# A bias tile of 32 columns instead of 64: every later tile of a cross-attention kernel moves down by 128 bytes

## What is computed

```python
q = _split_heads(hidden_states @ w_q, HEADS)
k = _split_heads(text @ w_k, HEADS)
v = _split_heads(text @ w_v, HEADS)
out_text = _merge_heads(_sdpa(q, k, v))
k_ip = _split_heads(ip_h @ w_k_ip, HEADS)
v_ip = _split_heads(ip_h @ w_v_ip, HEADS)
out_ip = _merge_heads(_sdpa(q, k_ip, v_ip, mask=mask_ip))
out = (out_text + IP_SCALE * out_ip) @ w_out + b_out
out = out + residual
```

## Time and profile before

| what | before |
|---|---|
| median of 3 runs | 918.4 us |
| lowest and highest run | 918.04 and 919.05 us |
| profiled execution: device time | 918.04 us |
| profiled execution: span from first to last instruction | 916.2 us |
| TensorE busy / VectorE busy / ScalarE busy / GpSimd busy | 97% / 80% / 66% / 57% |
| mean granted share of TensorE's clock | 0.992 |

### The profile page before, as it was taken

The page is one execution under the profiler, slowest core; times in us unless marked ns, Lnnn a source line. Parts: engine busy times, 40 slices in busy tenths (PEclk is TensorE's granted clock), DMA queues, the critical chain, the costliest instruction groups (busy, mean ns, idle before and its releaser), DMA issues.

```text
span 916.2 us, 13827 instructions
## 1 busy us (share of the span) xinstructions
PE 884.4 (97%) x4685; PEld 752.8 (82%) x4685; DVE 728.9 (80%) x999; ACT 605.3 (66%) x982; POOL 525.1 (57%) x422
## 2 busy tenths in 40 slices
PE   7999879999999999999999999999999999999967
PEld 7978758888888888888888888888888888888846
DVE  6494888888797978888897979787887879797772
ACT  4465767685858577676858586775768485866651
POOL 3372647566483928475664839284756648392731
PEclk9999999999999999999999999999999999999979
DMA  8685020303030110303030301203030303010101
GB/s 278 204 278 175 23 72 1 123 1 129 1 122 1 53 75 0 122 0 129 0 122 0 119 10 40 82 0 129 0 122 0 129 0 113 1 58 1 38 20 58
DMA packets 34151, 64.79 MB, mean 71 GB/s; under 512 B 4428, under 2 KB 6604, under 8 KB 33996
## 3 DMA queue, kind: packets, MB, share of 16 engines
q1 hardware_dynamic: 32812, 61.82, 20.2%
q10 hardware_dynamic: 1312, 2.62, 0.9%
HBM read 40.84 MB, written 23.59 MB: 70 GB/s over the span
## 4 chain that ended last, share of the span: by engine, by line
PE 81%; DVE 5%; ACT 2%; POOL 1%; issue 1%; POOLq 0%; DVEq 0%
PE bank L105 22%; PE bank L107 22%; PE bank L106 22%; PE bank L874 7%; PE bank L883 4%; PE bank L884 4%; DVE o_raw L754 1%; DVE total L765 1%; DVE pT_lo L747 1%; POOL prob L552 1%; ACT oT_hi L672 0%; ACT pv_part L668 0%; DVE prob L552 0%; POOL prob L558 0%; DVE prob L558 0%
## 5 line engine op out<-in xcount | busy, mean ns | idle before, releaser
L619 POOL TENSOR_TENSOR oT_lo<-o_raw,oT_hi 128x512 fp32r<-128x512 f32 x80 | 103.1, 1289 | 248.1 <-ACT oT_hi L672 248.1
L558 POOL TENSOR_TENSOR prob<-prob,inv 128x1120 f32<-128x1120 f32 x124 | 169.8, 1401 | 8.5 <-DVE inv L767 8.5
L552 POOL TENSOR_TENSOR prob<-prob,top 128x1120 f32<-128x1120 f32 x124 | 174.6, 1438 | 0.0
L105 PE MATMUL bank<-xT_hi,wq_hi 128*128 128x512 f32 x400 | 163.5, 409 | 2.6 <-DVE qT_lo L137 2.6
L107 PE MATMUL bank<-xT_hi,wq_lo 128*128 128x512 f32 x400 | 157.2, 393 | 0.0
L105 PE MATMUL bank<-oT_hi,wo_hi 128*128 128x512 f32 x400 | 156.1, 390 | 1.1 <-POOL oT_lo L619 0.7
L106 PE MATMUL bank<-xT_lo,wq_hi 128*128 128x512 f32 x400 | 156.1, 390 | 0.0
L106 PE MATMUL bank<-oT_lo,wo_hi 128*128 128x512 f32 x400 | 155.9, 390 | 0.0
L107 PE MATMUL bank<-oT_hi,wo_lo 128*128 128x512 f32 x400 | 155.6, 389 | 0.0
L754 DVE TENSOR_TENSOR o_raw<-bank,pv_part 64x512 f32<-64x512 f32 x160 | 110.2, 689 | 49.3 <-ACT pv_part L668 45.4
L759 DVE TENSOR_REDUCE top<-prob 128x20 f32<-128x1120 f32 (+1 forms) x128 | 98.8, 814 | 43.7 <-POOL prob L607 43.4
(11 more groups left out here) (88 smaller groups left out, 1741.3 us busy)
## 6 DMA issues: line engine op xcount, KB each, us to landing
outT<-res SPq DMA_DIRECT2D x80, 256.0 KB, 6.7
xin<-in_xT SPq DMA_DIRECT2D x14, 1280.0 KB, 6.8
w_raw<-in_L_xattn_w_v SPq DMA_DIRECT2D x8, 320.0 KB, 4.3
w_raw<-in_L_xattn_w_k SPq DMA_DIRECT2D x8, 320.0 KB, 3.6
w_raw<-in_L_xattn_w_v_ip SPq DMA_DIRECT2D x8, 320.0 KB, 3.8
w_raw<-in_L_xattn_w_k_ip SPq DMA_DIRECT2D x8, 320.0 KB, 3.8
xin<-in_xT ACTq DMA_DIRECT2D x2, 1280.0 KB, 7.4
v_raw<-v_scratch SPq DMA_DIRECT2D x16, 160.0 KB, 4.3
```

The lines of the kernel that those rows point to most:

```text
L105: nc.tensor.matmul(dst, a_hi, b_hi, start=first, stop=False)
L552: ins = eng.tensor_tensor(s, s, top[:, t, n, :].unsqueeze(2).broadcast_to([P, HEADS, k1 - k0]), ALU.subtract)
L558: ins = eng.tensor_tensor(s, s, inv[:, t, n, :].unsqueeze(2).broadcast_to([P, HEADS, k1 - k0]), ALU.mult)
L619: nc.gpsimd.tensor_tensor(oT_lo[:, m, :], o_raw[:, m % 2, :], oT_hi[:, m, :].bitcast(F32), ALU.subtract).then_inc(oT_lo_done, 1)
```

## The change

`LINE` goes from 64 to 32. It is used once, as the width of `bias`, so `bias` takes 128 bytes of each partition instead of 256, and each tile behind it starts 128 bytes lower.

```diff
@@ -33,7 +33,7 @@
 GRID = 32
 GQ = 512
 GT = GQ // P
-LINE = 64
+LINE = 32
 RING = 4
 LOADS = 6
```

## The result

| | before | after |
|---|---|---|
| median of 6 runs | 918.37 us | 923.74 us |
| lowest and highest | 917.51, 919.05 | 923.10, 924.72 |
| ratio after / before, 95% interval | | 1.0057 (1.0047 to 1.0067) |
| span of the profiled execution | 916.2 us | 922.5 us |
| distance of two output matmuls, mean | 227.1 ns | 232.5 ns |

The forecast was 918.3 us in a range of 916.4 to 920.6. The change costs 5.4 us by the medians and 6.3 us by the two profiled spans.

The account below looks back on a forecast made before the run. The prediction took TensorE, busy in 97% of the span, to bound the kernel. Its terms, 0 + 0 + 0 + 0, left the profiled 918.04 us at 918.0; it took 918.3 us for the median, range 916.4 to 920.6.

Parts of the forecast that it names:

- What bounds the kernel: Whole kernel: TensorE works in 97% of the span, with gaps only in the first 6 us and at both group ends.
- The streamed tile: 1520 TensorE matmuls streaming moved oT and pT: new address costs 0, bounds 21 us less or 21 us more.
- a fixed cost of a matmul: Reading of the 14.5 or 12.3 ns each TensorE matmul takes on top of its columns: it stays after the change.
- a cost of starting in the middle of a 256-byte piece: Other reading of those 14.5 or 12.3 ns per TensorE matmul: they go when the streamed tile starts at 0 modulo 256.
- The two-run row: Setup matmul streaming two 128-column runs, each starting at 128 modulo 256: 0.12 and 0.11 us, so the start costs nothing.
- The loaded tile: 640 transposes loading prob and 320 matmuls loading v_parts: 0, from setup loads at four addresses modulo 256 reading 0.17 to 0.18 us.
- VectorE, ScalarE, GpSimd: 0: Steps of these engines on moved tiles: 0, small operands worth 2 or 3 ns, ScalarE bounded at 3%.
- transfers: 0: Loads and stores of res, w_raw, ctx_raw and v_raw: 0, with bounds of 0.6 us on both sides.
- TensorE's streams get slower: Rival: a few ns more on 1520 streaming steps; 3 ns would be 4.6 us, 923; chance 4%.
- The first rival, cheaper streams: 14 ns less on 1520 streaming TensorE steps, 21 us, 897 us; or 2 to 5 ns, 915 to 911; chance 8% together.
- How the numbers follow: Chances for the whole kernel: 79% all terms below 0.2% together, 11% faster, 10% slower; range leaves out TensorE's stream cases, 12%.
- What would show it: Signs: output matmuls still 0.228 us apart if right; 0.215 or 0.24 with queries unchanged for an address cost on TensorE.

Follow-up runs that it names:

- kernel 1: Kernel before with 128-byte pads around oT, so only oT starts at 0 modulo 256 instead of 128: 924.05 us, ratio 1.0063.
- kernel 3: Kernel before with bias 32 columns and 128-byte pads before wq_hi and res, main-block tiles from wq_hi on at 0 modulo 256: 919.72 us, ratio 1.0012.
- kernel 5: Changed kernel's layout behind bias, with wo also moved to 0 modulo 256, so oT and wo are both at 0: 917.84 us, ratio 0.9996.
- kernel 13: Kernel before with only the loaded tile wo moved to 0 modulo 256, other main-block tiles at 128: 922.70 us, ratio 1.0052.
- kernel 12: Kernel before with bias 32 columns and a pad before k_hi, streamed k at 0 modulo 256, loaded qT at 128: 917.69 us, ratio 0.9996.
- kernel 11: Kernel before with 128-byte pads before and behind oT_lo, so only oT_lo moves to 0 modulo 256: 922.36 us, ratio 1.0045.
- kernel 16: Kernel before with oT_hi and oT_lo as halves of one tile, read from 4 bytes behind its start: 930.38 us, ratio 1.0138.
- kernel 8: Kernel before with oT at 64 modulo 256, 64 bytes behind wo: 924.27 us, ratio 1.0061.
- kernel 7: Kernel before with oT 64 bytes higher, at 192 modulo 256, 64 ahead of wo: 924.54 us, ratio 1.0069.

## Why the prediction was wrong, point by point

**What bounds the kernel** held. The loop is TensorE's, and what is added to a TensorE step there comes out at the end: 6.5 us by the steps, 6.3 us by the span.

**The streamed tile: the step that failed.** It counted the output's steps rightly and named two outcomes for them, "a fixed cost of a matmul" or "a cost of starting in the middle of a 256-byte piece", and took the first. Both are properties of one tile. The cost is one of two tiles, the streamed and the loaded (kernels 1, 3, 5, 13), and the 14 ns that looked as if they might be a price go with the cheap case, since in the kernel before every matmul of 512 columns in the main block had its two tiles at equal phases. The two-run row answered the question that was asked, whether a start at phase 128 costs something by itself, and answered it rightly. No row of before could have answered the other one. The term was put at 0 and should have been 1200 x 5.4 ns = 6.5 us, and for the 320 values matmuls 0, as their two tiles moved together: their mean distance to the next matmul went from 232.2 to 232.1 ns. The count left out 120 matmuls of the setup's keys, which stream `ctxT`; at the 0.7 ns each that the two traces differ by they are 0.1 us.

**The loaded tile.** The earlier trace rows do show loads at four phases under a stream at phase 128, and they cost nothing. It was read as a general answer. It is an answer for a stream of 320 columns; for 256 kernel 12 says the same, for the 640 transposes 0 was right (108.7 ns both times), and for 512 it is false. A duration of a load was also the wrong thing to read: in the changed kernel the loads of `wo` still take 188 ns or so, and it is the distance that is longer.

**VectorE, ScalarE, GpSimd: 0**, and **transfers: 0.** Right. The rows above have the same means, TensorE's first matmul comes after 6.3 us instead of 6.1, and kernel 2, which moves all of those tiles and not `oT`, is at 1.0006 (0.9995 to 1.0017).

**The rivals.** "TensorE's streams get slower" was the one that came true, in its place and nearly at its time: it said 3 ns on 1520 steps, 4.6 us and 923; it is 5.4 ns on 1200 steps and 923.7. That the time comes so near is luck: the price is nearly twice as high and the steps are fewer, and the cause it named, the moved stream alone, is not the one. It had 4% with the remark that no row spoke for it. None spoke against it either. The first rival, cheaper streams, did not happen: no layout tried settled under 226.7 ns. The Trainium skill ("TensorE: Matmul & The Clock Gate", Part 2, Back-to-back issue gap) gives 215.8 ns for bf16 at 512 columns; the 11 ns above it were there in every layout tried here, so none of these layouts removes them.

**How the numbers follow: the second step that failed.** The term was bounded at 21 us on either side because nothing in the trace measured it, and then the range was drawn at +2.3 us. With a bound that wide and an unknown sign, the forecast's 79% had no rows behind them. A third of the text's own upper bound, 7 us, would already have put the range past the 923.7 us that were measured.

**What would show it.** The list had the right line: output matmuls at another distance "with those of the queries unchanged". It put it down to the phase of the streamed tile, and kernel 3 shows that this reading would have been wrong too.

**Left open.** The medians differ by 5.4 us where the steps make 6.5. Executions at the same granted clock differ by more: at 0.996 the mean is 923.39 us after (14 executions) and 916.96 before (5), 6.4 us; at 0.994 it is 924.04 after (7) and 918.04 before (53), 6.0 us. So over these executions, from several rounds, the change costs nearly what the steps make, and the 5.4 us are what six against six happened to give. Kernels 11, 13 and 16 are also about 1 us cheaper than their distances. In the trace of kernel 13 the output's rows are 5.9 us longer than before, and the queries' rows 1.6 us shorter: in before half of the clock was granted for 3.4 us from 113.5 us on, in kernel 13 all of it between 93 and 139 us. At equal granted clock it still is only 5.0 to 5.4 us above before, so a part stays open.

Why a pair at unequal phases takes 5 ns longer is not shown, nor why it shows in streams of 512 columns and hardly or not at all in those of 128, 256 and 448. What is shown is where the short, settled distance of 226.7 ns comes: at equal phases of the two tiles.

## What to carry to other kernels

A tile's start address can be a term of TensorE's time: where a long row of 512-column float32r matmuls bounds a kernel, keep the streamed and the loaded tile at the same address modulo 256, and after any edit of a small tile in front of them look at the distance of two matmuls again. Padding a small tile so that the big ones behind it keep their phase costs 128 bytes of each partition and was worth 0.6% here. When a change only moves addresses, ask of each pair of tiles that are read together whether both moved, and give an effect that no row measures its full bounds in both directions.

## What was not expected of the hardware

- The distance of back-to-back float32r matmuls of 512 columns with a load between each settles on 226.7 ns when both tiles have the same start modulo 256 (227.1 in the mean), and is 231.7 to 233.4 ns in the mean at differences of 16, 32, 64 and 128 bytes. At 128 it was tried with either of the two moved, 232.5 and 232.3 ns. Shifting the streamed tile by 256 bytes changes nothing.
- At a difference of 64 bytes most rows settle too, but on 233.3 ns (all groups of kernel 8, 12 of 16 of kernel 7); three groups of kernel 7 run at 229.0 with the same addresses. At 128 the row runs through a pattern of seven values from 228 to 241 ns.
- At 256 columns the mean stays at 120 ns and at 128 at 108.7; at 448 it is 203.2 ns at equal phases, 203.9 at a difference of 128 bytes and 205.6 at 32 (kernel 13).
- A streamed tile that starts 4 bytes off a multiple of 16 costs 10.8 ns a step (237.9 against 227.1), where 16 bytes off the loaded tile cost 4.6.
- The Trainium skill ("TensorE: Matmul & The Clock Gate", Part 2, Step-by-step, LDWEIGHTS) says that TensorE has two SBUF read ports and that loading the next weights takes no read bandwidth from the running matmul. As to ports and bandwidth no run here speaks. But the loads are not without effect on the matmuls beside them: the address of the loaded tile alone changes their distance, from 227.1 to 232.3 ns (kernel 13).
